# The mask of a biased attention: added by TensorE for 83 of 128 pairs of units, by GpSimd for 45

## The reference

```python
# attention of layer 3, for each of the 4 sequences and 16 heads of 16 features
scores = jnp.einsum('bhqd,bhkd->bhqk', q / math.sqrt(HEAD_DIM), k)
scores = scores + attention_bias              # (4, 16, 512, 512), float32
scores = jnp.where(src_mask, -jnp.inf, scores)   # mask (4, 1, 512, 512)
probs = jax.nn.softmax(scores, axis=-1)
ctx = jnp.einsum('bhqk,bhkd->bhqd', probs, v)
```

## Time and profile before

| | us |
|---|---|
| median of 3 runs | 1169.03 |
| lowest and highest | 1167.12, 1172.2 |
| the profiled execution, its own time | 1163.56 |
| its span, from first to last instruction | 1161.5 |
| PE, DVE, ACT, POOL busy | 997.7, 730.8, 694.2, 454.1 |

### The profile page before, as it was taken

The page is one execution under the profiler, slowest core; times in us unless marked ns, Lnnn a source line. Parts: engine busy times, 40 slices in busy tenths (PEclk is TensorE's granted clock), DMA queues, the critical chain, the costliest instruction groups (busy, mean ns, idle before and its releaser), DMA issues.

```text
span 1161.5 us, 22288 instructions
## 1 busy us (share of the span) xinstructions
PE 997.7 (86%) x7668; PEld 658.7 (57%) x7668; DVE 730.8 (63%) x1964; ACT 694.2 (60%) x1608; POOL 454.1 (39%) x694
## 2 busy tenths in 40 slices
PE   4878889897889898798889998897996899799768
PEld 3435557465556575466546565575573557557545
DVE  5677773737755738846773668638649864764750
ACT  3566564664675755676565755656754775675731
POOL 8300020000530374561072006847737564894920
PEclk8899999998999998899999999899897899999989
DMA  6868425133261634854626128575393387944600
GB/s 175 224 157 187 74 73 113 34 84 62 63 140 46 146 122 127 198 177 149 130 75 148 37 90 209 183 166 194 104 226 104 121 225 224 219 141 150 214 1 19
DMA packets 118354, 154.79 MB, mean 133 GB/s; under 512 B 12956, under 2 KB 80924, under 8 KB 118244
## 3 DMA queue, kind: packets, MB, share of 16 engines
q1 hardware_dynamic: 113636, 147.04, 47.3%
q0 software_dynamic: 1936, 3.97, 1.4%
q10 hardware_dynamic: 2672, 2.36, 0.6%
HBM read 134.47 MB, written 18.88 MB: 132 GB/s over the span
## 4 chain that ended last, share of the span: by engine, by line
PE 51%; DVE 18%; ACT 15%; issue 9%; DMA 4%; POOL 4%; DVEq 0%; ACTq 0%; POOLq 0%
PE bank L1307 14%; PE bank L1296 9%; PE bank L1399 7%; PE bank L1258 5%; PE bank L1413 5%; PE bank L1381 4%; POOL bias L798 4%; DMA bias<-in_fside_Bx16xSxS 3%; DVE mrow L1142 3%; ACT gT L874 3%; DVE bias L1148 3%; ACT bias L827 2%; ACT prob L824 2%; ACT L874 2%; ACT L827 2%
## 5 line engine op out<-in xcount | busy, mean ns | idle before, releaser
L798 POOL TENSOR_TENSOR bias<-bias,negmask 128x256 f32<-128x256 f32 x512 | 335.9, 687 | 259.2 <-DMA bias<-in_fside_Bx16xSxS 252.6
L827 ACT ACTIVATE bias<-bias,mrow 128x512 f32<-128x512 f32 x256 | 184.1, 719 | 209.3 <-DVE mrow L1148 207.8
L1148 DVE CUSTOM_DVE_ANT_0 bias<-bank,bias 128x512 f32<-128x512 f32 x256 | 175.4, 687 | 186.5 <-PE bank L1381 175.3
L824 ACT ACTIVATE prob<-bank,mrow 128x128 f32<-128x128 f32 (+3 forms) x256 | 134.7, 527 | 193.1 <-DVE mrow L1142 191.6
L1142 DVE TENSOR_REDUCE mrow<-bank 128x1 f32<-128x128 f32 (+3 forms) x256 | 124.5, 488 | 164.5 <-PE bank L1384 163.1
L1381 PE MATMUL bank<-ks,qs 128*128 128x512 bf16 (+3 forms) x512 | 180.3, 352 | 49.2 <-ACT prob L824 34.5
L1399 PE MATMUL bank<-ident,bias 128*128 128x128 f32 x1024 | 164.7, 286 | 54.0 <-ACT pT L835 43.8
L1399 PEld LDWEIGHTS bank<-ident,bias 128*128 128x128 f32 x1024 | 125.2, 146 | 123.9 <-ACT bias L827 71.3
L1296 PE MATMUL bank<-hT,w 128*128 128x512 f32 x384 | 182.6, 606 | 2.0 <-ACT hT L851 0.9
L1307 PE MATMUL bank<-w,gT 128*128 128x256 f32 x768 | 174.3, 381 | 0.0
L1307 PEld LDWEIGHTS bank<-w,gT 128*128 128x128 f32 x768 | 142.5, 190 | 20.2 <-issue 2.7
(11 more groups left out here) (155 smaller groups left out, 1140.6 us busy)
## 6 DMA issues: line engine op xcount, KB each, us to landing
bias<-in_fside_Bx16xSxS SPq DMA_DIRECT2D x128, 512.0 KB, 4.6
w<-in_L_cond_W SPq DMA_DIRECT2D x16, 1024.0 KB, 5.6
qs<-q_parts SPq DMA_DIRECT2D x30, 384.0 KB, 10.3
ks<-k_parts SPq DMA_DIRECT2D x30, 384.0 KB, 11.7
q_parts<-parts SPq DMA_DIRECT2D x80, 128.0 KB
k_parts<-parts SPq DMA_DIRECT2D x48, 128.0 KB
w<-in_L_cond_Wi SPq DMA_DIRECT2D x4, 1024.0 KB, 5.0
w<-in_L_cond_Wo SPq DMA_DIRECT2D x4, 1024.0 KB, 5.6
```

What stands on the lines that cost most here:

```text
L798: pool.tensor_tensor(b_n, b_n, negmask[:, t, keys], ALU.add).then_inc(masked, 1)
L824: act.activation(prob_of(U), score_bank[U % 2][:, 0:n], ACT.Exp, bias=mrow[:, U % ROW_RING:U % ROW_RING + 1], accum_out=rsum[:, U % ROW_RI ...
L827: act.activation(prob_of(U), prob_of(U), ACT.Exp, scale=-1.0, bias=mrow[:, U % ROW_RING:U % ROW_RING + 1], accum_out=rsum[:, U % ROW_RING: ...
L1148: v.tensor_tensor_reduce(out=prob_of(U), in0=score_bank[U % 2][:], in1=prob_of(U), scale=-1.0, scalar=3e38, op0=ALU.add, op1=ALU.min, accu ...
```

## The change

```diff
+PE_LOAD = {"turn_tokens": 9, "qk": 17, "v": 17, "project": 17, "hidden": 17, "ff_out": 34, "turn_expert": 2, "down": 9, "expert": 5,
+           "up": 9}
+PE_MASK_UNDER = 5
+def mask_sides():
+    load = {}
+    for t, e, step, _ in EVENTS:
+        if e == "pe":
+            load[t] = load.get(t, 0) + PE_LOAD.get(step, 0)
+        elif e[0] == "v":
+            load[t] = load.get(t, 0) - V_LOAD.get(step, 0)
+    sides = []
+    for a in BIASED:
+        for U in range(UNITS * a, UNITS * (a + 1), 2):
+            sides.append(sum(load.get(t, 0) for t in range(U - 3, U + 5)) < 8 * PE_MASK_UNDER)
+    return sides
+ON_PE = mask_sides()
+POOL_PAIRS = [n + 1 - sum(ON_PE[:n + 1]) for n in range(len(ON_PE))]
...
-                pool.wait_ge(masked, PIECES * (n + 1))
+                pool.wait_ge(masked, PIECES * POOL_PAIRS[n])
...
+                        if BIASED[V // UNITS]:
+                            before = max(x for x in BIASED if x < V // UNITS)
+                            pool.wait_ge(s_psum, UNITS * before + UNITS // 2 + 2 * GH * (t + 1))
                         mask_term(NT * ATTENTIONS[V // UNITS][0] + t)
-                    mask_pair(bias_pair(V), t)
+                    if not ON_PE[bias_pair(V)]:
+                        mask_pair(bias_pair(V), t)
...
-                    if j % 2 == 0:
-                        v.wait_ge(masked, PIECES * (bias_pair(U) + 1))
+                    p = bias_pair(U)
+                    if j % 2 == 0 and ON_PE[p]:
+                        v.wait_ge(bias_in[p % BIAS_RING], 16 * (p // BIAS_RING + 1))
+                    elif j % 2 == 0:
+                        v.wait_ge(masked, PIECES * POOL_PAIRS[p])
...
+                on_pe = l == 1 and ON_PE[bias_pair(U)]
                 mm = pe.matmul(score_bank[U % 2][:, 0:n], qs[:, hd, t * P:(t + 1) * P], ks[:, hd, 0:n],
-                               start=True, stop=l == 1)
+                               start=True, stop=l == 1 and not on_pe)
+                if on_pe:
+                    pe.wait_ge(mask_neg, 2 * (NT * ATTENTIONS[a][0] + t + 1))
+                    mm = pe.matmul(score_bank[U % 2][:], identb[:], negmask[:, t, :], start=False, stop=True)
```

## The result

The changed kernel takes 1149.54 us (median of 4 runs, 1148.26 to 1150.45) against 1168.07 us for the kernel before (4 runs, 1167.0 to 1172.2). The ratio is 0.9837, with a 95% interval from 0.9813 to 0.9861: 18.5 us less, where 6.3 were forecast. The direction was right. The size was not, and the time lies 0.5 us under the range.

What follows compares the result with a forecast made beforehand. No engine was taken as full: DVE set the pace in three stretches, POOL or nearly so in two. The sum -17.0 + 12.7 - 2.0 = -6.3 us gave 1162.7 us from 1169.03, range 1150 to 1176.

Steps and rivals of the forecast that it cites:

- The gain from DVE's slowed steps: DVE steps on the chain, slowed beside POOL's additions for PE pairs, return to usual length: 10.9 us gained.
- The waits for POOL: DVE no longer waits for POOL's additions: 2.6 us at a late pair and 3.5 in 979 to 1029 us.
- the late pair: Bias landed at 708.5 us, DVE began behind POOL's four additions at 711.2: 2.6 us gained.
- The wait of 3.04 us: DVE's first wait at the start of attention 7, given nothing because PE's projection covers it.
- POOL's pace at the end: Last 24 units of attention 7 run at POOL's 1.28 us each; without POOL they would take 1.18.
- The masks' forecast there: End of attention 7: with masks 1.33 us a unit, 0.05 more than now, for 30 units: 1.5 us cost.
- The masks: Added matmuls cost 0.22 us each where on the path: 7.0 + 4.2 + 1.5 = 12.7 us.
- The rival in which PE takes over: Two thirds of 166 masks on the path make the kernel slower, 1176 us; chance 0.16.
- The clock: Fuller PE clock in 432 to 488, 687 to 743 and 863 to 932 us gives back 2.0 us.
- as the rival said: Low-clock stretches vanish and 6.7 us come back in full, giving 1158 us; chance 0.24.
- The rival in which DVE's slow steps remain: The 45 remaining POOL pairs still slow DVE beside norms; 5.5 us lost, 1168 us, no visible change; chance 0.18.

Runs made afterwards that it cites:

- e3: The changed kernel, with GpSimd still making the additions for the 65 PE pairs of attentions 5 to 7, on a dead tile nobody reads: 1163.38 us.
- e5: The changed kernel without the 166 mask matmuls, with GpSimd's unused additions for the 65 PE pairs of attentions 5 to 7: 1156.81 us.
- e1: The changed kernel without the 166 mask matmuls, so the 83 PE pairs get no mask from anyone: 1139.75 us.
- e9: The kernel before, with the mask on TensorE for pairs 10 to 19 of attention 3 alone: 1165.23 us.
- e10: The kernel before, with the mask on TensorE for the 15 PE pairs 68 to 83 of attention 6 alone: 1157.98 us.
- e11: The kernel before, with the mask on TensorE for pairs 96 to 104 of attention 7 alone: 1166.39 us.
- e8: The changed kernel with each of the 166 mask matmuls made twice: 1164.35 us.
- e7: The changed kernel, with PE pairs 0 to 2, 27 to 37, 91 to 95, 113 to 127 back on GpSimd and 20 to 22, 61 to 63 on TensorE: 1140.34 us.
- e6: The changed kernel with PE pairs 0 to 2, 27 to 37, 91 to 95 and 113 to 127 given back to GpSimd: 1147.81 us.

## Why the prediction was wrong

Read from the timelines, from the first DVE step of one pair to that of another, the change in us against the trace of before (attention 3 has no dummy additions in e3 and e5):

| pairs | after | e1 | e3 | e5 |
|---|---|---|---|---|
| 11 to 19 | -4.2 | -5.1 | -4.4 | -5.0 |
| 27 to 32 | +2.2 | 0.0 | +1.8 | +0.1 |
| 32 to 38 | +1.3 | 0.0 | +1.3 | 0.0 |
| 38 to 45 | -4.6 | -6.2 | -1.8 | -1.7 |
| 68 to 75 | -9.2 | -8.7 | -1.0 | -0.4 |
| 75 to 82 | +0.8 | -0.7 | +3.2 | +1.4 |
| 96 to 100 | -2.6 | -3.2 | -2.4 | -3.2 |
| 113 to 127 | +1.8 | -0.4 | +2.3 | -0.4 |

**The gain from DVE's slowed steps: the mechanism right, the size wrong.** The step that failed is the sentence "Slowed steps off the chain I count at nothing, because DVE has idle time there." With it the prediction took 10.9 us, and 17.0 with the waits. e1 measured 28.9 for the same removal, and its DVE is busy 27.7 us less. e3 and e5 show that the additions alone are worth 13.8 and 17.1 us for 65 of the 83 pairs, at most 3.3 of it by waits for the pairs that POOL keeps, and that each slowed microsecond counts for 0.8 to 1. The other 12.2 us that e5 has under the kernel before are in its trace 6.3 in attention 3 (pairs 0 to 3 and 11 to 19), where nothing was added back, and 4.9 of waits (pairs 38 to 45 and 96 to 100). In 432 to 488 the prediction had no gain at all, only 2.2 us of masks; pairs 11 to 19 gained 4.2, and e9 4.6 in the same stretch, though e9's whole time does not settle it. e10 gained 9.2 us where the prediction's own terms for the stretch come to 4.7. The likely reason is that a chain of waits is one path: where PE and DVE wait for each other every unit, a slowed step that is not on the drawn path is on one nearly as long. That reason is argued; the price is measured.

**The waits for POOL: about right in the traces, open in the whole time.** 2.6 us for the late pair and 3.5 for attention 7 were forecast. The wait of 3.04 us was indeed covered in part by PE's projection; pairs 96 to 100 gave 2.6, pairs 96 to 105 together 2.7, and 3.7 in e1, without masks. As a whole-kernel time, e11's 0.8 us leaves it open between nothing and 3.2. In e5, where pairs 38 to 45 keep the additions but not the wait, 1.7 us are left.

**POOL's pace at the end: wrong.** The prediction took the 1.28 us a unit of the last 24 for POOL's pace and expected 1.18 without it. In e1 those units have neither POOL's additions nor a mask. The last 32 units, as in the earlier trace rows:

```profile
1044.50:1053.90 9.40, 5.55 (x16) 1.00 0.98 332
1053.90:1084.30 30.40, 15.89 (x47) 1.00 0.48 155
```

That is 30.4 us for 30.8, or 1.27 a unit. The drawn chain ran over POOL there, but something else was as slow; what it was stays open. The masks' forecast there came near what was measured although its premise was false.

**The masks: a little too dear.** 12.7 us were forecast, 9.8 measured (e1). Where DVE is full they are free (pairs 68 to 75), where PE is full or the units run alone they cost: 1.3 us for 12 units from 32 to 38, 0.11 each, and at the end 1.8 over before, 2.2 over e1, for 28 units, 0.08 each. The forecast for the end was 1.5 for 30. The step of 0.22 itself was right, 0.23 in the chain above; fewer lie on the path. The Trainium skill ("TensorE: Matmul & The Clock Gate", "Back-to-back issue gap") gives 131 ns for a sustained stream. No run here shows it: in e8 the second mask starts 0.216 us behind the first. The count behind the forecast has a slip: its groups outside the end add up to 104 masks, not 107, and 32 more (pairs 83, 91 to 95 and 96 to 104, and one pair of attention 5) have no price. The rival in which PE takes over has fallen: even twice the masks (e8) do not reach the time of before.

**The clock: too small, and not a term of its own.** 2.0 us were forecast. In the three stretches the time at 1.2 GHz went from 40 us to 2 x 0.03 x 54 = 3, as the rival said, and in the whole kernel from 95 to 48. But it follows DVE: e5 has it low again (0.81 in pairs 68 to 75) with no mask, and raising it by masks alone (e3, 0.91) brings 0.6 us there, their own cost taken off. In a stretch where PE is full, 3.4 us at half clock cost 0.9. That the clock was lower where PE was less busy, as the prediction read it, does not come out of the earlier trace rows: PE is busy 79% at a clock of 0.85 in 863 to 932 and 78% at 1.00 in 1070 to 1109.

**The rival in which DVE's slow steps remain** was wrong for the PE pairs and right for six POOL pairs that the change had left beside norms: e7 moves them and gains 7.5 us over e6. In the traces e7 is 4.1 us ahead of e6 from pair 11 to 19 and 3.1 from 45 to 64, with 8.9 and 7.2 us less of POOL's work there, since POOL had made those additions ahead of time. The 2.1 us by which attention 4 differs, with its half clock, come on top, and e6's profiled execution was 3.1 us over its median.

The ends of the range were drawn from the same 17.0 us. With e1's 28.9 in its place and the masks as forecast the sum would have been -16.2; with e1's 9.8 for the masks too it is -19.1, for 18.5 measured; that the last two agree says nothing, since 28.9 less 9.8 is by construction the kernel before less the changed one. The direction was not luck, since slowed steps were named as the largest gain; that the sum still fell to a third of the measured one is mostly that term.

## What to carry to other kernels

Compare each instruction's duration with the median of its own line before looking at any wait: an engine that is off the path can lengthen another's steps, and it is booked on the victim. Such excess counted for 0.8 to 1 of its length here, on the drawn chain or not; the chain shows one path of several, and what it names as the limit need not be the only one. Then move work by where its neighbour is slowed, not by where it is itself waited for: 55 pairs, chosen by what the first experiments showed, beat 83 by 9.2 us, and 128 were no better than 83.

## What the runs showed of the hardware

A DVE instruction on 4 columns took 3.03 us beside a run of GpSimd additions, for 0.16 alone, and a 512-column sum 2.70 for 0.69; the steps that read a bank in PSUM kept their time, as L1148 in the trace of before, lowest, median and highest in ns:

```profile
L1148 DVE CUSTOM_DVE_ANT_0 bias<-bank,bias x256: 671/691/693, 382.7 to 1108.8; 128x512 f32<-128x512 f32 x128
```

166 matmuls of 512 columns more, beside GpSimd's additions, left the time at 1166.71 against 1168.7 us, with gains and losses by stretch. In the changed kernel they cost 0.06 us each on average, for 0.22 of their own time.

In a stretch where TensorE is full, 3.4 us at half clock cost 0.9 us (e7) and 6.8 us cost 3.0 (e6).
